# Where the low halves of q and k are made in an L1-distance attention: on VectorE, or by a second product on TensorE

## The reference, cut to what matters

```python
v = (x @ wqv_w.T + wqv_b).reshape(b, t, 3 * h, d)          # h = 8 heads, d = 64
q, vf, vb = (v[:, :, :h], v[:, :, h:2 * h], v[:, :, 2 * h:])
k = x[:, :, None, :] * wk[None, None]
# a[s, t, head] = -sum_w |q[s, head, w] - k[t, head, w]| / 8, all pairs of tokens
a = jax.nn.softmax(concat(a, zeros), axis=1)[:, :t]
o = (einsum(a, vf) + einsum(a^T, vb)).sum(heads)
y = o * sigmoid(1.702 * o);  return x + (y @ fanin_w.T + fanin_b)
```

## Time and profile before

| | before |
|---|---|
| median of 3 runs | 2817.27 us |
| profiled execution | 2817.37 us, span 2815.6 us |
| busy share: TensorE, VectorE, ScalarE, GpSimd | 76%, 82%, 49%, 62% |
| L1 attention's pairs | about 714 to 2628 us of the span |

### The profile page before, as it was taken

How to read it: one execution, slowest core, us unless ns; L and a number is a source line. 1 busy time by engine, 2 the same in 40 slices (tenths; PEclk the granted TensorE clock), 3 DMA queues, 4 the chain that set the end, 5 groups by cost and what they waited for, 6 DMA issues and landing times.

```text
span 2815.6 us, 43219 instructions
## 1 busy us (share of the span) xinstructions
PE 2145.3 (76%) x11861; PEld 898.4 (32%) x11861; DVE 2322.0 (82%) x2847; ACT 1380.3 (49%) x2997; POOL 1750.9 (62%) x1015
## 2 busy tenths in 40 slices
PE   4649999994777777777777777777777777777466
PEld 3533333331223223223223323223222232232245
DVE  3877778788889889889899899899899899898542
ACT  0325555552455555555555555555555555555234
POOL 0103333232588888887887887887887887887411
PEclk8879999997899999999999999999999999999768
DMA  5100000000111111111111111111111111111000
GB/s 136 44 1 1 1 0 0 0 0 2 49 44 47 46 41 46 47 42 45 47 43 43 47 45 43 47 46 43 45 47 43 44 47 44 43 47 46 16 11 19
DMA packets 163208, 101.96 MB, mean 36 GB/s; under 512 B 55773, under 2 KB 161182, under 8 KB 163039
## 3 DMA queue, kind: packets, MB, share of 16 engines
q1 hardware_dynamic: 162858, 101.41, 14.6%
q10 hardware_dynamic: 316, 0.12, 0.0%
HBM read 10.63 MB, written 4.19 MB: 5 GB/s over the span
## 4 chain that ended last, share of the span: by engine, by line
PE 47%; DVE 29%; issue 16%; ACT 3%; DVEq 2%; DMA 1%; SPq 1%; POOL 1%; ACTq 0%; POOLq 0%
DVE score L1337 21%; PE pp L744 14%; PE pp L593 5%; DVE qk L1316 3%; PE pp L715 3%; PE pp L686 2%; PE pp L614 2%; PE pp L672 2%; PE pp L618 2%; PE pp L615 2%; PE pp L619 2%; PE pp L679 2%; PE pp L585 1%; PE pp L710 1%; ACT vb L966 1%
## 5 line engine op out<-in xcount | busy, mean ns | idle before, releaser
L1337 DVE TENSOR_REDUCE score<-pp 128x16 f32<-128x1024 f32 x1408 | 1644.1, 1217 | 192.5 <-PE pp L744 189.4
L1452 POOL TENSOR_TENSOR absd<-absd 128x2560 f32<-128x2560 f32 (+4 forms) x640 | 1450.1, 2266 | 368.0 <-ACT absd L977 327.9
L744 PE MATMUL pp<-blocks,pick 128*128 128x512 f16 x4096 | 1111.6, 382 | 199.5 <-DVE score L1337 161.8
L977 ACT ACTIVATE absd<-pp 128x1024 f32<-128x1024 f32 x640 | 655.0, 1023 | 712.7 <-PE pp L744 712.7
L744 PEld LDWEIGHTS pp<-blocks,pick 128*128 128x128 f16 x4096 | 316.2, 98 | 852.3 <-DVE score L1337 464.1
L1428 POOL TENSOR_TENSOR absd<-absd,yw 128x512 f32<-128x512 f32 x112 | 142.3, 1270 | 318.9 <-DVE yw L1255 318.9
L916 ACT ACTIVATE absd<-pp 128x512 f32<-128x512 f32 x256 | 150.8, 596 | 148.2 <-PE pp L615 145.7
L1271 DVE SCALAR_TENSOR_TENSOR absd<-pp,absd 128x512 f32<-128x512 f32 x256 | 172.4, 687 | 53.2 <-ACT absd L916 38.6
L989 ACT ACTIVATE expd<-attn 128x65 f32<-128x65 f32 x512 | 155.6, 315 | 0.0
L593 PE MATMUL pp<-absd 128*64 128x512 f32 x512 | 138.1, 618 | 0.0
L672 PE MATMUL pp<-wk_diag,xT 96*128 96x512 f32 x130 | 74.1, 652 | 73.0 <-DVE qk L1316 73.0
(11 more groups left out here) (200 smaller groups left out, 2201.8 us busy)
## 6 DMA issues: line engine op xcount, KB each, us to landing
blocks<-qk SPq DMA_DIRECT2D x1032, 64.0 KB, 2.0
attn<-score SPq DMA_DIRECT2D x1024, 16.0 KB, 1.8
xs<-xn SPq DMA_DIRECT2D x66, 32.0 KB, 1.8
big<-in_wrb_t SPq DMA_DIRECT2D x1, 2064.0 KB
big<-in_x_rows SPq DMA_DIRECT2D x4, 512.0 KB, 6.2
token_rows<-big SPq DMA_DIRECT2D x8, 256.0 KB, 2.0
big<-in_L_ffn_w SPq DMA_DIRECT2D x4, 512.0 KB, 10.0
out<-big SPq DMA_DIRECT2D x16, 128.0 KB, 2.0
```

The lines of the kernel that those rows point to most:

```text
L744: mm = pe.matmul(ps[bank + n], pick[:, unit % 8 + n, :], blocks[:, b, unit // 16, unit // 8 % 2, :], start=True, stop=True)
L977: nc.scalar.activation(absd[odd][:, 16 * u:16 * u + 16, :], pp[:, 4:6, :].rearrange("p n (h w) -> p (n h) w", w=D), ACT.Abs).then_inc(X["a ...
L1337: dve.tensor_reduce(score[:, odd, b, 16 * d:16 * d + 16], pp[:, bank:bank + 2, :].rearrange("p n (h w) -> p (n h) w", w=D), AX.X, ALU.add, ...
L1452: nc.gpsimd.tensor_tensor(x[:, :, 0:w], x[:, :, 0:w], x[:, :, w:2 * w], ALU.add).then_inc(X["tree"], 1)
```

## The change

The low half is no longer made by VectorE. TensorE waits for the high half, makes the same f32 product again into `ps[6]`, and adds to it a second, f16 product of the high half with `neg_eye`, a 128x128 matrix with -2048 on the diagonal. ScalarE then copies the bank to the low f16 tile. `neg_eye` is made once by VectorE. In `extra`, `turn` goes from after unit 7 to after unit 8, `queries` from after 9 to after 10, the new `low` of q is put after unit 12 of image 0 and that of k after unit 0 of image 1. `finish` on VectorE goes from after the reduce D4 to after D3.

```diff
+        neg_eye = sb("neg_eye", [P, P], F16)
 ...
@@ TensorE
-            pe.wait_ge(X["consts"], 2)
+            pe.wait_ge(X["consts"], 3)
+            def low(p, odd, kind):
+                pe.wait_ge(X["half"], 4 * p + 2 * kind + 1)
+                if kind:
+                    pe.matmul(ps[6], xT1[:, odd, :], wk_diag[:].rearrange("p h d -> p (h d)"), start=True, stop=False)
+                else:
+                    pe.matmul(ps[6], xTq[:], wqv[:, 0:QK], start=True, stop=False)
+                pe.matmul(ps[6], neg_eye[:], qk[:, kind, 0, :], start=False, stop=True).then_inc(X["klo_ps" if kind else "qlo_ps"], 1)
 ...
-                        if k == 7:
+                        if k == 8:
                             turn(q + 1, at)
-                        if k == 9:
+                        if k == 10:
                             queries(q + 1, at)
+                        if k == 12:
+                            low(q + 1, 1 - odd, 0)
                         if k == 14:
                             keys(q + 1, 1 - odd)
                     else:
+                        if k == 0:
+                            low(q + 1, 1 - odd, 1)
 ...
@@ ScalarE
+            def low(p, kind):
+                act.wait_ge(X["klo_ps" if kind else "qlo_ps"], p + 1)
+                nc.scalar.copy(qk[:, kind, 1, :], ps[6]).then_inc(X["half"], 1)
 ...
                 high_q(q + 1, False)
+                low(q + 1, 0)
                 absolute(s, 0, 4, first)
                 s += 1
                 high_k(q + 1)
+                low(q + 1, 1)
                 absolute(s, 1, 0, first)
 ...
@@ VectorE
+            dve.tensor_scalar(neg_eye[:], ident[:], -LO_SCALE, None, ALU.mult).then_inc(X["consts"], 1)
 ...
-            def low(p, kind):
-                dve.wait_ge(X["half"], 4 * p + 2 * kind + 1)
-                dve.scalar_tensor_tensor(out=qk[:, kind, 1, :], in0=qk[:, kind, 0, :], scalar=-LO_SCALE, in1=ps[6],
-                                         op0=ALU.mult, op1=ALU.add).then_inc(X["half"], 1)
 ...
-                        if b == 0 and d == 4 and at >= 3:
+                        if b == 0 and d == 3 and at >= 3:
                             finish(q - 3, slot)
-                        if b == 0 and d == 8:
-                            low(q + 1, 0)
-                        if b == 1 and d == 1:
-                            low(q + 1, 1)
```

More of the change, by code:

```diff
@@ L264, in build @@
         X = {n: sem("d_" + n) for n in (
-            "xs", "wk_in", "consts", "xT_ps", "xT_sb", "xTq", "q_ps", "k_ps", "half", "tb0", "tb1",
+            "xs", "wk_in", "consts", "xT_ps", "xT_sb", "xTq", "q_ps", "k_ps", "qlo_ps", "klo_ps", "half", "tb0", "tb1",
             "diffD", "diffA", "red", "abs", "tree", "pooled", "spread0", "spread1", "exp", "zr", "attk", "attq_ps", "attq",
@@ L777, in _ @@
             queries(0, 0)
+            low(0, 0, 0)
             keys(0, 0)
+            low(0, 0, 1)
             for q in range(4):
@@ L1040, in _ @@
             high_q(0, True)
+            low(0, 0)
             high_k(0)
+            low(0, 1)
             for q in range(4):
@@ L1359, in _ @@
             dve.wait_ge(X["hx"], 1)
-            low(0, 0)
-            low(0, 1)
             for q in range(4):
```

## The result

The changed kernel takes 2710.68 us (median of 4 runs, 2709.4 to 2712.7) against 2817.17 us (4 runs), a ratio of 0.9622 with a 95% interval of 0.9606 to 0.9639: 106.5 us less. Forecast were 2708 us and a range of 2688 to 2770. The profiled execution took 2712.7 us with a span of 2710.9, the slowest of the four; its span is 104.7 us under that of before.

A forecast was written before the change was run, and what follows sets the result against it. It took VectorE's chain, with holes made by in-order TensorE, as the bound. From 2817.37 us, -113 for 61 pairs, -3 for the first three and +4.5 at the start gave 2706, with rounding 2708; range 2688 to 2770.

The forecast's parts named there:

- What bounds the kernel: Pair loop: VectorE's chain, 26.5 us of work in a 30.01 us period, with 3.5 of holes made by in-order TensorE.
- the layout by hand: One period of the pair loop laid out instruction by instruction in the new order; it gave a period of 28.16 us.
- Removed, moved, added: Per pair: 1.20 us off VectorE, turn's hole of 0.92 + 0.09 gone, TensorE 2.2 to 2.4 more, ScalarE 2 x 0.60.
- cross-check: Pair period summed a second way: 25.3 us of VectorE work plus 2.9 of listed holes make 28.2.
- The split into work and holes: Pair loop: VectorE's work goes from 26.5 to 25.3 us a pair, its holes from 3.5 to 2.9.
- The unknown price: At each low, an f16 matmul added to an f32 product: 0.86 + 0.22 us taken, 1.51 at most, 48 us in all.
- A sign that was off: Among the signs to show the forecast right: VectorE busy by about 88 us less.
- The start: Before the first pair: lows run in line on TensorE at the 1.2 GHz clock, +4.5 us, bounds +2 to +6.
- Rival 1: Image 0's last six units: small products bunch up, one hole of 1.01 us a pair returns, 2770 us; chance 0.10.
- Rival 2: At the lows: TensorE's new work displaces all VectorE sheds, 2830 or 2818 us; with rival 3, 0.06 slower, 0.03 same.
- Rival 3: At the lows: TensorE stands waiting for ScalarE's high half, 2830 us; shares 0.06 slower, 0.03 same with rival 2.
- Rival 4: Pair loop: the four new holes, 1.01 us a pair together, don't appear, 27.15 a pair, 2646 us; chance 0.05.

The follow-up runs named there:

- lows alone: Changed kernel with turn, queries and finish back at their old places, the lows staying on TensorE: 2799.51 us, ratio 0.9941.
- the run with a later ScalarE: Changed kernel with one more ScalarE copy ahead of the high copy of q and of that of k: 2774.5 us, ratio 0.9852.
- the run without the second product: Changed kernel without the repeated f32 product, the low tile being the neg_eye product alone: 2656.34 us, ratio 0.9429.
- the run with the old start: Changed kernel with vb copied before A0's absolute value, and the first pair's two lows on VectorE again: 2657.76 us, ratio 0.9437.

## Why the prediction was right

**What bounds the kernel** held: VectorE's chain with holes made by TensorE's order. Seven of the eight runs came within 6 us of what the layout by hand gave, the eighth (lows alone) within 10.

**Removed, moved, added.** The period was forecast as 28.16 to 28.2 and is 28.25. Held against the layout (its times less 10.16, plus 1500): D7's reduce 1518.97 forecast and 1519.01 measured, D9 1521.46 and 1521.61, D10 1522.82 and 1522.98, D1' 1525.41 and 1525.48, D7' 1532.77 and 1532.85. The 0.15 at D9 is a mis-sized term: the high half of q is ready at 1519.32, not 1519.20, so low q starts 0.05 later and its product takes the 0.96 of one that waited instead of 0.86. ScalarE's copy, not TensorE's queue, has the last word there, which the run with a later ScalarE confirms. Low k was mis-sized the other way: it was given the 0.97 of a product that waits and took 0.86, which is why the hole before D1' is 0.14 and not 0.24. The cross-check's hole of 0.07 before D3' does not follow from the layout (35.57 and two reduces of 1.13 are 37.83, against 37.84), and there is none in the trace; the period of 28.16 does not rest on it.

**How near the time came.** The profiled span, less the 2.55 us ahead of the stage, is 107.2 below before. The 60 periods and what follows them gave 108.3 where 113 was forecast, the first three pairs 3.3 for 3, and the start took 4.4 for 4.5. So the terms missed by 4.3 us, and the 2 us that had been added for rounding happened to cover half of it. Two slips in the range change nothing here: its terms (-7, and -2.5 for the start) give 2698, not 2696, as the low end, and its chance stands once as 0.76 and once as 0.70.

**The split into work and holes.** The prediction split the gain of a period into 1.20 of work and 0.6 of holes, and the trace adds up so: 1.20 and 0.56. As a split by causes it fails: alone, the lows' move brings 0.33, the places 0.76, and 0.67 comes only with both. The lows' 1.20 came through in full in the run without the second product, with the moves in place and no f32 product added.

**The unknown price** (an f16 product added to an f32 one): taken at 0.22 and measured at 0.22 of TensorE's time (1520.33 to 1520.55), the end of the range that I took. The upper end, 0.4 a low, didn't show.

**A sign that was off**: VectorE's busy time was to fall by 88 us and fell by 65 on the page (2322.0 to 2256.8). The lows' printed 0.68 overlap the next reduce by 0.09, so 130 of them free 78 us, not 88, and each of the two further holes of a period adds 0.09 to a printed reduce, some 11 us in all. The price of 0.60 used in the sum was the right one.

**The start**: +4.5 forecast, +4.4 in the trace, and as much given back by the run with the old start. `neg_eye` stood 8.30 us beside GpSimd's 8.80 and the scaling behind it took 0.41, where alone in that place it had taken 8.50: the weights were ready 0.1 later in all. So the row of 8.50 was a wait for GpSimd, not a price of scaling: whichever scaling stood there first ended with GpSimd, and the same instruction behind it took 0.41. The trace agrees with what the Trainium skill (SBUF — State Buffer, SBUF: two separate sides) says of the port pair that GpSimd shares with VectorE's two-port operations: the one that comes second is blocked for the other's whole instruction.

**The rivals.** Rival 1 (the gain of the moved `turn` is lost) is out: in the changed kernel the moves are worth 1.43 a pair (29.68 with the lows alone, 28.25 with both), and without the lows 0.76. Rival 2 (displaced in full) is out by the result and by the run without the second product: 0.80 of 1.82 counts. Rival 3 names a real mechanism that does not set in here: 0.53 us more in front of each high copy costs 0.99 a pair, and by that price (an estimate) both high halves would have to be about 0.9 late to lose the gain of 1.76, as the prediction has it. Rival 4 (no new holes) is out: 0.16, 0.25, 0.15 and 0.14 are there, where 0.13, 0.14, 0.14 and 0.24 had been laid out, printed as idle time.

## What to carry to other kernels

Where several in-order engines feed each other, work taken off the busiest engine is worth what the next engine has ready for it; lay out one period with start-to-start prices from the timeline and read the gain from the holes, before and after. Look at each hole for the one instruction that stands in front of the unit that is late: moving `turn`, the vb copy and a third of attend by one or two places brought 0.76, 0.77 and 0.45 us a pair and added no work. Test a new wait by delaying what it waits for: if nearly the whole delay comes through, as 0.99 of 1.06 did here, an engine with 40% of idle time sets the pace there.

## What the runs showed of the hardware that was not expected

In the run with the moves alone TensorE's granted clock fell in six pairs, and such a pair took 0.5 to 0.7 longer: in every fifth from the one that begins at 916 us to the one that begins at 1503, and once more in the one at 2265. The stretches of such a pair (columns as in the earlier trace rows), and TensorE just ahead of the fall:

```profile
928.00:930.00 2.00, 0.94 (x2) 0.40 (x3) 2.00 (x3) 0.04 (x1) 1.88 (x1) 1.00 0.10 25
930.00:932.00 2.00, 2.00 (x7) 0.68 (x5) 1.25 (x2) 0.60 (x1) 2.00 (x1) 0.56 0.10 25
932.00:934.00 2.00, 2.00 (x7) 0.58 (x6) 1.79 (x3) 1.02 (x1) 1.92 (x2) 0.58 0.26 64
934.00:936.00 2.00, 1.18 (x8) 0.59 (x7) 2.00 (x3) 1.03 (x1) 2.00 (x1) 1.00 0.40 97
```

```profile
925.42 1.56 PE L744 MATMUL pp<-blocks,pick 128*128 128x512 f16 x6
927.34 0.60 PE L744 MATMUL pp<-blocks,pick 128*128 128x512 f16 x2 [0.35 <-DVE score L1337]
929.06 1.13 PE L672 MATMUL pp<-wk_diag,xT 96*128 96x512 f32 x2 [1.12 <-DVE qk L1316]
930.02 4.48 PE L744 MATMUL pp<-blocks,pick 128*128 128x512 f16 x12
```

The clock is 0.56 and 0.58 in two stretches, most of each at the 1.2 GHz level (0.50), and back at 2.4 GHz (1.00) in the next. Ahead of it TensorE had worked 0.94 of 2 us, between the holes of 0.35 and 1.12. The same places in the pair that begins at 945 have the same two holes (0.35 before 957.12, 1.12 before 958.84) and the clock stays at 1.00 there, so the fall depends on more than the pair's own order; what decides it was not settled. In the loops of the kernel before, the changed kernel and the other seven experiments it shows 1.00.
